# A four-layer graph network on one core: loads reordered, another beginning, sixteen split-tile slots, later projections of s and d

## What is computed

```python
x = layernorm(x + L0(x))  # L0: adj @ (x W0) + b0
x = layernorm(x + L1(x))  # L1: graph attention, 4 heads; ht = x W1 (256 -> 4*256)
                          #     src = ht . a_src, dst = ht . a_dst, e = leaky_relu(src_i + dst_j) + adj
                          #     mean over heads of softmax(e) @ ht
x = layernorm(x + L2(x))  # L2: two graph convolutions with W1, W2
x = layernorm(x + L3(x))  # L3: relu(adj_norm @ x @ W)
```

## Time and profile before

| | |
|---|---|
| time, median of 3 runs | 686.25 us (685.97 to 686.39) |
| time of the profiled execution | 686.31 us |
| its span | 684.6 us |
| PE busy | 673.4 us |
| PE, first work of its own (L556) | at 4.91 us |
| PE, first matmul of s and d (L546) | at 78.89 us |

### The profile page before, as it was taken

One profiled execution on the slowest core, in us unless ns is written; L12 is line 12 of the kernel. 1 busy time (PEld: TensorE's weight loads), 2 busy tenths in 40 slices (PEclk: granted clock), 3 DMA queues, 4 the chain that ended last, 5 costly groups with the idle time before them and its releaser, 6 DMA issues.

```text
span 684.6 us, 14405 instructions
## 1 busy us (share of the span) xinstructions
PE 673.4 (98%) x5326; PEld 512.5 (75%) x5326; DVE 521.6 (76%) x965; ACT 388.8 (57%) x499; POOL 166.2 (24%) x260
## 2 busy tenths in 40 slices
PE   8989999999999999999999999999999999999996
PEld 6878744888888888888888888884444468886444
DVE  4257668998998989989899898999454425874685
ACT  6556448898979889898898979643101000222000
POOL 4369717601000000000100001664021102442222
PEclk9999999999999999999999999999999999999998
DMA  8999431003003030030300303013021111211011
GB/s 307 402 407 300 85 105 37 16 1 82 13 33 61 27 65 0 31 61 31 61 0 31 61 0 63 1 37 72 17 54 24 24 23 17 40 39 32 32 51 42
DMA packets 48153, 47.65 MB, mean 70 GB/s; under 512 B 36016, under 2 KB 42224, under 8 KB 45936
## 3 DMA queue, kind: packets, MB, share of 16 engines
q1 hardware_dynamic: 45664, 39.37, 19.0%
q0 software_dynamic: 2016, 7.34, 5.7%
q10 hardware_dynamic: 432, 0.39, 0.2%
HBM read 29.23 MB, written 2.13 MB: 46 GB/s over the span
## 4 chain that ended last, share of the span: by engine, by line
PE 93%; DMA 4%; ACT 1%; DVE 1%; POOL 0%; issue 0%; SPq 0%; ACTq 0%; POOLq 0%
PE ps L720 17%; PE ps L722 16%; PE ps L721 16%; PE ps L566 16%; PE ps L556 9%; PE ps L669 6%; PE ps L568 6%; PE ps L569 6%; DMA arena<-in_adj 4%; ACT adj L408 1%; DMA arena<-in_x_turned 1%; PE ps L546 0%; DVE x L784 0%; POOL rstd L1182 0%; DVE total L894 0%
## 5 line engine op out<-in xcount | busy, mean ns | idle before, releaser
L722 PE MATMUL ps<-arena,ring_hl 128*128 (+1 forms) x1024 | 279.7, 273 | 0.0
L720 PE MATMUL ps<-arena,ring_hl 128*128 (+1 forms) x1024 | 278.9, 272 | 0.0
L721 PE MATMUL ps<-arena,ring_hl 128*128 (+1 forms) x1024 | 278.6, 272 | 0.0
L1043 DVE SCALAR_TENSOR_TENSOR ring_a<-rho,gam,ring_a 128x1024 f32<-128x1024 f32 x128 | 164.9, 1288 | 18.0 <-ACT ring_a L463 18.0
L1048 DVE TENSOR_TENSOR ring_hl<-ring_a,ring_hl 128x1024 f16<-128x1024 f32 x128 | 157.2, 1229 | 4.9 <-ACT ring_hl L477 4.8
L477 ACT ACTIVATE ring_hl<-ring_a 128x1024 f16<-128x1024 f32 x128 | 135.2, 1056 | 43.6 <-PE ps L722 29.2
L463 ACT ACTIVATE ring_a<-adj,shift 128x1024 f32<-128x1024 bf16 x128 | 145.6, 1138 | 0.0
L568 PE MATMUL ps<-arena,adj 128*128 128x257 f16 (+1 forms) x512 | 113.1, 273 | 2.6 <-ACT adj L408 2.6
L569 PE MATMUL ps<-arena,adj 128*128 128x256 f16 x512 | 113.1, 273 | 0.0
L566 PE MATMUL ps<-arena,adj 128*128 128x512 f16 x496 | 111.6, 379 | 0.0
L721 PEld LDWEIGHTS ps<-arena,ring_hl 128*128 128x128 f16 x1024 | 99.1, 97 | 13.8
(11 more groups left out here) (109 smaller groups left out, 589.3 us busy)
## 6 DMA issues: line engine op xcount, KB each, us to landing
arena<-in_adj SPq DMA_DIRECT2D x16, 1024.0 KB, 10.9
x<-y POOLq DMA_DIRECT2D x14, 512.0 KB, 5.2
rho<-s_scratch SPq DMA_DIRECT2D x8, 512.0 KB, 3.7
x<-in_x SPq DMA_DIRECT2D x4, 512.0 KB, 16.3
out_x<-x SPq DMA_DIRECT2D x16, 128.0 KB, 1.7
arena<-in_x_turned SPq DMA_DIRECT2D x2, 512.0 KB, 7.5
arena<-in_L_gnn_W SPq DMA_DIRECT2D x1, 1024.0 KB, 10.6
arena<-in_L_gnn_a SPq DMA_DIRECT2D x1, 1024.0 KB, 12.5
```

Of the source, the lines that this page charges most:

```text
L720: nc.tensor.matmul(acc, hi, v_hi, start=(jt == 0), stop=False)
L721: nc.tensor.matmul(ps[:, b, 0:D], hi, v_lo, start=False, stop=False)
L722: ins = nc.tensor.matmul(acc, lo, v_hi, start=False, stop=(jt == T - 1))
L1043: nc.vector.scalar_tensor_tensor(a, rho[:, q, :], gam[:, at(h, 1), jt], a, op0=ALU.max, op1=ALU.mult)\
```

## The change

It has these parts: (a) eight more warm-up matmuls; tile 1 of the transposed x is loaded by ACT's queue, and tiles 2 and 3 by a load of their own; (b) turned high parts are issued in another order, two of them by DVE; DVE casts pieces 0 and 2 later; (c) PE begins the aggregation piece by piece; (d) W1 and a are loaded behind adjacency piece 9, the third quarter of x behind them and the last behind piece 11; (e) `xg` has sixteen slots, the second eight in the buffer of `rho`; (f) on ACT casts and W1's high parts move, on DVE and POOL products, their sums and `was` move to later tiles and the bias is added one tile ahead; (g) each share of s and d comes behind a half value tile in place of ahead of it, and tile 15's a half later; DVE takes value tile 2 before s and d.

```diff
-    WARM = 28
+    WARM = 36
-        XT_LOADS = [(0, 1), (1, 4), (4, 6), (6, 8), (8, 12), (12, 16)]
+        XT_LOADS = [(0, 1), (1, 2), (2, 4), (4, 6), (6, 8), (8, 12), (12, 16)]
...
             load_x(1)
+            load_adj(6)
+            load_adj(7)
+            load_adj(8)
+            load_adj(9)
             sp.wait_ge(s_lo, T)
             sp.dma_start(w1f, ...)
             sp.dma_start(abc..., ...)
-            load_adj(6)
-            load_adj(7)
             load_x(2)
-            load_adj(8)
-            load_x(3)
-            for n in range(9, NL - 2):
+            for n in range(10, NL):
                 load_adj(n)
-            for n in range(NL - 2, NL):
-                load_adj(n)
+                if n == 11:
+                    load_x(3)
...
             act.dma_start(w0f[:, 0, :], w0r[:, 0, :]).then_inc(ld_w0[0], 16)
+            act.dma_start(xts[:, 1:2, :], xt_in[:, 1:2, :]).then_inc(ld_xt[1], 16)
...
-            for n in (1, 3, 4, 5):
+            for n in (1, 3, 4, 5, 6, 7):
                 cast_n(n)
-            w1_hi(0)
-            w1_hi(1)
-            cast_n(6)
-            behind = {0: [(CAST, 7)], 2: [(CAST, 8)], 3: [(CAST, 9)], 4: [(CAST, 10)], 5: [(CAST, 11)], 6: [(CAST, 12)],
-                      7: [(CAST, 13)], 9: [(CAST, 14)], 10: [(CAST, 15)], 12: [(was_hi,)]}
+            behind = {n - 5: [(CAST, n)] for n in range(8, NL)}
+            behind[5].append((w1_hi, 0))
+            behind[6].append((w1_hi, 1))
+            behind[13] = [(was_hi,)]
...
-            joint(0, 0, lambda t: 0, columns_cast)
+            for t in range(T):
+                project(0, t, t % R)
+            pe.wait_ge(s_one, 1)
+            for n in FIRST_LOADS:
+                pe.wait_ge(*cast_done(n))
+                for j in range(n % 2 * JH, (n % 2 + 1) * JH):
+                    if n < 2:
+                        pe.wait_ge(s_c, j + 1)
+                    for it in (n // 2 * 2, n // 2 * 2 + 1):
+                        agg_step(0, 0, it, it, j, j == T - 1)
...
             pe.wait_ge(s_wl, 2)
-            pe.wait_ge(s_was, 1)
+            pe.wait_ge(*turned(1, 0))
             for n, share in enumerate(shares):
-                for t in share:
-                    project(1, t, t % R)
                 if n < R:
                     pe.wait_ge(s_sum, T - R + n + 1)
                 values_half(n // 2, n // 2, n % 2)
+                if n == 0:
+                    pe.wait_ge(s_was, 1)
+                for t in share:
+                    project(1, t, t % R)
             values_half(3, 3, 0)
             values_half(R, 0, 0)
+            values_half(R, 0, 1)
             project(1, T - 1, R - 1)
-            values_half(R, 0, 1)
+            values_half(R + 1, 1, 0)
             pe.wait_ge(s_c, 2 * T)
...
-            casts_after = {8: 0, 11: 2}
+            casts_after = {11: 0, 15: 2}
...
-            fill = {t: [lambda t=t: sum_products(t - R)] for t in range(R, R + 4 * K2)}
-            fill[8].append(lambda: weight_lo(1, w1, w1ff, [0]))
-            fill[9].append(lambda: weight_lo(1, w1, w1ff, [1]))
-            fill[13] = [was_lo]
+            fill = {t: [lambda t=t: sum_products(t - 7)] for t in range(7, 7 + 4 * K2)}
+            fill[10].append(lambda: weight_lo(1, w1, w1ff, [0]))
+            fill[12].append(lambda: weight_lo(1, w1, w1ff, [1]))
+            fill[15] = [was_lo]
...
-            for t in range(T + 2):
+            for t in range(T + 1):
                 if t < T:
                     inv_std(t, t % R)
-                if t >= 2:
-                    prep_lo(1, t - 2, (t - 2) % R, x)
-                if 0 <= t - 2 < 4 * K2:
-                    product(t - 2)
-                if R <= t < T - R:
-                    add_b0(t + R)
+                for n in (t - 2,) if t < 14 else (12, 13) if t == 14 else (t - 1,):
+                    if n >= 0:
+                        prep_lo(1, n, n % R, x)
+                if 2 * R <= t + 1 < T:
+                    add_b0(t + 1)
+                if 0 <= t - 6 < 4 * K2:
+                    product(t - 6)
```

More of the change, by code:

```diff
@@ L143, in graph_stack @@
         prod = part(a_flat, (2 * CH, 2 * CH + H * D), F32, "p (h f) -> p h f", h=H)
-        xg = part(y[:, :, :].rearrange("p a f -> p (a f)"), (0, BANKS * D), F16, "p (s q f) -> p s q f", s=BANKS, q=2)
+        xg = [part(v, (0, BANKS * D), F16, "p (s q f) -> p s q f", s=BANKS, q=2)
+              for v in (y[:, :, :].rearrange("p a f -> p (a f)"), r_flat)]
         sd_bank = ps[:, 7, 0:2 * 2 * H * T].rearrange("p (t b c) -> p t b c", t=T, b=2)
@@ L149, in graph_stack @@
         ld_x = [sem(f"ld_x{i}") for i in range(R)]
-        ld_xt = [sem(f"ld_xt{i}") for i in range(6)]
+        ld_xt = [sem(f"ld_xt{i}") for i in range(7)]
         ld_adj = [sem(f"ld_adj{i}") for i in range(STAGES)]
@@ L251, in _ @@
             for n, (lo, hi) in enumerate(XT_LOADS):
-                sp.dma_start(xts[:, lo:hi, :], xt_in[:, lo:hi, :]).then_inc(ld_xt[n], 16)
+                if n != 1:
+                    sp.dma_start(xts[:, lo:hi, :], xt_in[:, lo:hi, :]).then_inc(ld_xt[n], 16)
                 if n == 0:
@@ L289, in _ @@
                 sp.dma_start_transpose(xt[:, t, :].rearrange("p (c i) -> p c i", c=2 * K2),
-                                       xg[:, t % BANKS, :, :].rearrange("p q f -> p (q f)")).then_inc(s_tc[t % 2], 16)
+                                       xg[t // BANKS][:, t % BANKS, :, :].rearrange("p q f -> p (q f)"))\
+                  .then_inc(s_tc[t % 2], 16)
             sp.wait_ge(s_cap, 1)
@@ L394, in _ @@
             w0_hi(1)
-            for chunk in CHUNKS[1:6]:
-                turned_hi(*chunk)
-            turned_after = {0: 6, 1: 7, 3: 8, 5: 9}
+            turned_hi(*CHUNKS[1])
+            turned_hi(*CHUNKS[2])
+            turned_after = {0: CHUNKS[3:5], 1: CHUNKS[5:6], 2: CHUNKS[6:7], 3: CHUNKS[7:8]}
             for t in range(T):
                 take_p(0, t, t % R)
-                if t in turned_after:
-                    turned_hi(*CHUNKS[turned_after[t]])
+                for chunk in turned_after.get(t, []):
+                    turned_hi(*chunk)
             for n, bi in enumerate((b1_in, b2_in)):
@@ L415, in gat_hi @@
                 act.wait_ge(s_norm, t + 1)
-                if t >= BANKS:
-                    act.wait_ge(*turned(1, t - BANKS))
-                nc.scalar.activation(xg[:, t % BANKS, 0, :], x[:, t, :], ACT.Copy).then_inc(s_hi, 1)
-            for n in (1, 3, 4, 5):
+                nc.scalar.activation(xg[t // BANKS][:, t % BANKS, 0, :], x[:, t, :], ACT.Copy).then_inc(s_hi, 1)
+            for n in (1, 3, 4, 5, 6, 7):
                 cast_n(n)
-            w1_hi(0)
-            w1_hi(1)
-            cast_n(6)
             CAST = cast_n
-            behind = {0: [(CAST, 7)], 2: [(CAST, 8)], 3: [(CAST, 9)], 4: [(CAST, 10)], 5: [(CAST, 11)], 6: [(CAST, 12)],
-                      7: [(CAST, 13)], 9: [(CAST, 14)], 10: [(CAST, 15)], 12: [(was_hi,)]}
+            behind = {n - 5: [(CAST, n)] for n in range(8, NL)}
+            behind[5].append((w1_hi, 0))
+            behind[6].append((w1_hi, 1))
+            behind[13] = [(was_hi,)]
             for t in range(T):
@@ L440, in value_hi @@
                     held_back = isinstance(t, int) and t == R - 1 and half == 1
-                    act.wait_ge(s_ht, t * 2 + (half + (4 if held_back else 1)))
+                    act.wait_ge(s_ht, t * 2 + (half + (5 if held_back else 1)))
                     nc.scalar.activation(
@@ L694, in _ @@
                              start=True, stop=True).then_inc(s_turn, 1)
-            values_half(R + 1, 1, 0)
+            values_half(R + 1, 1, 1)
             pe.wait_ge(s_sr, 1)
             values_half(3, 3, 1)
-            values_half(R + 1, 1, 1)
             tiles(pe, R + 2, T, values)
@@ L953, in turned_lo, with turned_hi @@
                 nc.vector.tensor_sub(xt[:, lo:hi, D:2 * D], xts[:, lo:hi, :], xt[:, lo:hi, 0:D]).then_inc(s_lo, hi - lo)
+            def turned_hi(lo, hi):
+                dve.wait_ge(s_hi, lo)
+                dve.wait_ge(*xt_loaded(lo))
+                nc.vector.tensor_copy(xt[:, lo:hi, 0:D], xts[:, lo:hi, :]).then_inc(s_hi, hi - lo)
             turned_lo(*CHUNKS[0])
@@ L958, in _ @@
                                                op0=ALU.mult, op1=ALU.subtract).then_inc(lo_made, 1)
-            for chunk in CHUNKS[1:5]:
-                turned_lo(*chunk)
-            casts_after = {8: 0, 11: 2}
+            turned_lo(*CHUNKS[1])
+            turned_lo(*CHUNKS[2])
+            casts_after = {11: 0, 15: 2}
+            turned_after = {3: 8, 5: 9}
             for t in range(T):
                 take(0, t, t % R)
+                if t == 0:
+                    turned_lo(*CHUNKS[3])
+                    turned_lo(*CHUNKS[4])
                 if t in casts_after:
                     cast_n(casts_after[t])
+                if t in turned_after:
+                    turned_hi(*CHUNKS[turned_after[t]])
```

(24 more changed lines are left out.)

## The result

The changed kernel takes 697.21 us (696.38 to 698.49, 4 runs) against 686.32 (685.97 to 687.09) for the kernel before in the same session: a ratio of 1.0163, 95% interval 1.0151 to 1.0175. It is slower by 10.9 us. The forecast was 693.8 us, or +7.5, in a range of 688.5 to 697.5. The profiled execution took 697.55 us, its span is 695.5.

What follows compares the result with a forecast made beforehand. The prediction took TensorE, busy 673.4 us, as the bound, other engines counting only where it waits. 686.31 + 5.9 (wait for `was`) + 2.0 (lower clock) - 0.3 (part (g)) = 693.9, median forecast 693.8 us, range 688.5 to 697.5.

Steps and rivals of the forecast that it cites:

- the upper bound: Latest `was`, 88.8 us: landings of a and pieces 6 and 7 2 us later, both meetings with W1's rest in full.
- the sum: The forecast's addition: 686.31 + 5.9 for the wait + 2.0 for the clock - 0.3 = 693.9 us.
- The beginning: Warm-up and first tiles: aggregation begins at 17.8 us, not 19.43; 1.6 us won, then lost in the wait for `was`.
- The loads: Order of DMA loads: early piece waits go, up to 2 us return at pieces 10 and 11, a lands at 47.8 us.
- the ring's term: GpSimd's turns with a product: 3.38 us plus VectorE's sum and aggregate and hand-overs, 4.3 us against TensorE's 3.5.
- The meetings with W1's rest: VectorE's bodies 10 and 12, beside GpSimd's small instructions: 0.4 us each, bounds 0 to 1.
- Turn 7: GpSimd's turn after the first product: begins at 50.8 us, the first of seven turns of 4.3 us.
- The clock: TensorE after the long wait for `was`: matmuls at 1.2 GHz for a while, costing 2.0 us, bounds 0 and 3.5.
- Rival 1: TensorE at `was`: the same wait, but the clock level is kept; 691.9 us, chance 0.18.
- Part (g): After tile 15's s and d: 1.31 us more matmuls cover the 0.4 us weight-load wait, -0.3 us.
- Rival 2: A longer wait: a lands, or pieces 6 and 7 are cast, 2 us or more later; 697 us, chance 0.10.
- Rivals 3 and 4: 3: GpSimd's turns don't stretch, 682.9 us, chance 0.13; 4: both effects cancel, no change that can be told, chance 0.04.

Runs made afterwards that it cites:

- e7: The kernel before with only the changed kernel's beginning, parts (a) to (c) and the order of VectorE's first bodies: 686.21 us, ratio 0.9997.
- e6: The changed kernel with the beginning of the kernel before, parts (a) to (c) undone: 698.70 us, ratio 1.0193 to the kernel before.
- e1: The changed kernel with VectorE's sum of a product moved behind the aggregate in its body: 692.23 us, ratio 1.008 to the kernel before.
- e2: The changed kernel with GpSimd's bias added two tiles ahead in place of one: 694.05 us, ratio 1.0107 to the kernel before.
- e5: The changed kernel without GpSimd's eight products and VectorE's sums of them, `wa` a constant: 688.88 us, ratio 1.0047 to the kernel before.
- e9: The changed kernel with VectorE's normalise and sum moved behind the aggregate in bodies 7 to 14, bias still one ahead: 688.69 us, ratio 1.005.
- e4: The changed kernel with 44 unread matmuls of 512 columns in front of TensorE's wait for `was`: 696.15 us, ratio 1.0133 to the kernel before.
- e8: The changed kernel with sum behind the aggregate, bias two tiles ahead and TensorE's wait for `was` behind two half value tiles: 683.52 us, ratio 0.9966.
- e10: The kernel before with GpSimd's bias for tiles 8 to 15 added one tile ahead in place of four: 697.85 us, ratio 1.0178.
- e3: The changed kernel with VectorE's sum behind the aggregate and the bias two tiles ahead: 684.94 us, ratio 0.9981 to the kernel before.

## Why the prediction was right and where it was off

*Direction, place and kind: right.* TensorE waits behind the first half value tile for `was`, GpSimd's turns are stretched with VectorE's aggregate as releaser, the clock falls. `was` came at 89.55 us, forecast 86.1. That is outside the bounds given for it, 82.7 to 88.8, though neither the loads nor a were 2 us late, which the upper bound assumed. The upper bound had no term for longer turns, and from the prediction's own terms (2 us, and 0.6 for each meeting) it would be 86.1 + 3.2 = 89.3. The time of 697.21 us is inside the range only because the clock cost less than its bound of 3.5; that it ends up within 0.3 us of the edge is luck and no support for the sum.

*The beginning (1.6 us won, lost again later): right.* It was 2.2 us in the profiled execution and 1.5 on average over all profiles; e7 shows that alone it moves nothing. "By the sum below they are worth nothing" holds within the 1.5 us that e6 leaves open.

*The loads: right in kind.* The prediction put 3.4 us on the waits for pieces in the kernel before; the row that it cites has 2.6, and the rest is the aggregation's own pace. Waits on casts 6 to 9 are gone, 1.1 and 1.0 us of wait stand before casts 10 and 11. A third, 1.1 us before cast 15, was not foreseen: that cast stands on ScalarE behind `gat_hi` of tile 10, which the ring delays. It cost nothing, since it lies in front of the long wait.

*The step that failed is the ring's term.* "So each turn with a product becomes 3.38 us of GpSimd plus the sum and the aggregate of VectorE ... 4.3 us." Measured are 4.63 (56.08 to 60.71). The forecast had VectorE's own side at 4.4 us with normalise at 0.67, that is, held only as in the earlier trace rows. What failed is the overlap: the sum let normalise and stats run beside the product. In its new place normalise starts while the product runs and ends 0.16 us behind it, so 0.3 us of stats and 0.1 of the hand-over come on top. e1, e2 and e5 take the parts away one by one: 4.15 without the sum, 4.32 without the tie to the bias, 3.62 without the product, and 3.37 with sum and tie both gone; e9, which only changes the order in the body, has 3.50. Seven turns of 0.32 us make 2.2 us of the miss.

*The meetings with W1's rest: 0.87 us each, not 0.4.* The turns that follow bodies 10 and 12 take 5.5 us (65.33 to 70.83). GpSimd's first small instruction there takes 1.08 us in place of 0.19: it begins 0.15 us behind VectorE's and ends with it.

```profile
65.18 1.19 DVE L988 SCALAR_TENSOR_TENSOR w<-arena,w 128x1024 f16<-128x1024 f32 x1
65.33 1.08 POOL L1195 TENSOR_TENSOR veps<-mv,epsv 128x1 f32<-128x1 f32 x1 [1.25 <-DVE mv L843]
```

This is 1.0 us of the miss. The prediction's sentence on the Trainium skill said that each meeting costs what is left of VectorE's instruction, and the traces agree; the sum did not follow it. The Trainium skill, "SBUF — State Buffer", section "Who interferes with whom", also counts `tensor_scalar`, which normalise is, among the VectorE instructions that can need the pair of ports shared with GpSimd, and says that the later of two such instructions is blocked until the first ends. The traces agree: normalise takes 0.95 us beside a product and 0.40 without.

*Turn 7 began at 51.46 (forecast 50.8), the last body was 0.4 us shorter.* Together +0.3 us. So 2.2 + 1.0 + 0.3 = 3.5 us, the whole distance from 86.1 to 89.6.

*The clock: 2.0 us forecast, 1.6 measured (e4).* Rival 1 is refuted, the granted clock was 0.50. That "the granted clock never leaves 1.00 on any row", which was put forward for that rival, was a weak sign; the last section says why.

*Part (g): 0.3 us of gain forecast, none seen, and the step was misread.* "1.31 us of matmuls more lie between tile 15's s and d and the turn of s": there was one half tile between them before (`values_half(R, 0, 1)`), and there is one after (`values_half(R + 1, 1, 0)`). The 0.4 us stayed as they were the earlier trace rows. A further 0.35 us lie outside the span (697.55 - 695.5 = 2.05 us against 1.71). It was 2.0 to 2.1 in all runs of e1 to e5, e8 and e9, 1.8 to 1.9 in e7 and in three of the four runs of e6, and 1.7 to 1.8 in the kernel before and in e10. So the beginning accounts for some 0.1 to 0.2 of it; what makes the rest stays open.

In sum: 9.4 (wait) + 1.6 (clock) + 0.35 - 0.1 for the rest = 11.2 us in the profiled execution. Rival 2 named nearly the measured time, 697, but by another way: a did not come late, the first product starts at 49.25 us without idle time before it, and `was` is late because of the turns. That its number fits is luck. Rivals 3 and 4 are refuted, the ring is there.

## What to carry to other kernels

Where two engines hand tiles to each other, write down for one turn which instruction of the one waits for which of the other, and follow the order of both programs until it closes: if the closed path is longer than the time that the bounding engine takes for a tile, the lag grows with each tile, and everything won before it is lost. Such a ring is opened by the distance of the hand-over (one tile ahead or two) or by the order in a body, at no cost seen here: 12.3 us lie between the medians of the changed kernel and e3, and 13.7 between it and e8. And take the duration of an instruction from a row in which the other engine does the same thing as in its new place.

## What the runs showed of the hardware that was not expected

A VectorE normalise (128 x 256, f32 to f32 in SBUF) took 0.95 us when it began 0.5 us into a GpSimd product of 1.28 us, 0.53 to 0.76 beside shorter ones (e3, e2), 0.40 beside none (e5), and 0.38 when it began 0.1 us before a product ended (e9). GpSimd's instruction on a single column took 1.08 us when begun 0.15 us behind VectorE's 1.19 us one on 1024 columns, and 0.18 to 0.27 otherwise. VectorE's addition of a PSUM tile (0.42 us, at 58.33) and its stats (0.43 us, in e9 at 59.77) ran beside the product at their usual length.

The granted clock fell to 0.50 around waits of TensorE of 3.6 us and longer (e9, e5, e1, e2 and the changed kernel), in e5 and e9 only after the work had begun again, and not behind the 1.6 us of e3. In e10 it fell 0.9 us after the end of a wait of 2.7 us.

In the rows the granted clock was given as 1.00 for the slow stretch at the beginning of the kernel before. That reading was not a measurement: the first record of the clock in this trace lies at 11.9 us, and the windows show 1.00 for what lies ahead of it. The matmuls there started 0.213 us apart, and 0.109 apart from 12.0 on. In e6, which has the same beginning, the records start sooner, at 3.7 us, and the same pace has its clock beside it:

```profile
8.00:9.00 1.00, 1.00 (x7) 0.50 1.02 307
11.00:12.00 1.00, 0.68 (x7) 1.00 0.98 414
```

So at the beginning of these traces the pace of the matmuls is the better witness.
